# A relational graph layer on one core: the first weight's scale split in two halves, and its first half moved ahead of x's second tile

## The reference

```
h = relu(layernorm(x))                               # 1250 x 1024
u = h @ root + bias + sum over r of mean_r(h[src] by dst) @ weight[r]     # 8 relations
z = concat(u, h) @ w_gate + b_gate
out = x + tanh(u) * z + h * (1 - z)
```

## Time and profile before

| | us |
|---|---|
| median of 3 runs | 1406.08 |
| the three runs | 1405.66, 1406.08, 1414.51 |
| span of the profiled execution, from its first to its last instruction | 1407.7 |
| PE busy | 1291.5 (92%) |
| DVE busy | 952.5 (68%) |
| POOL busy | 754.8 (54%) |
| ACT busy | 409.0 (29%) |

### The profile page before, as it was taken

How to read it: one execution, slowest core, us unless ns; L and a number is a source line. 1 busy time by engine, 2 the same in 40 slices (tenths; PEclk the granted TensorE clock), 3 DMA queues, 4 the chain that set the end, 5 groups by cost and what they waited for, 6 DMA issues and landing times.

```text
span 1407.7 us, 20144 instructions
## 1 busy us (share of the span) xinstructions
PE 1291.5 (92%) x6205; PEld 651.6 (46%) x6205; DVE 952.5 (68%) x1260; ACT 409.0 (29%) x501; POOL 754.8 (54%) x837
## 2 busy tenths in 40 slices
PE   2978899999999999999998999998999989786898
PEld 1434344444444445555554445454445445343565
DVE  6889678366565667775675577646666778765777
ACT  5344123214132422321332043223222323432000
POOL 2423088786878426686687558664756464320000
PEclk9998899999999999999999999999999999998999
DMA  6442125215224348777875887769889977648872
GB/s 220 154 173 101 44 52 156 69 45 171 54 59 122 114 158 277 238 237 247 277 209 161 292 267 246 238 210 305 279 254 303 312 230 240 204 138 248 239 226 90
DMA packets 112355, 269.44 MB, mean 191 GB/s; under 512 B 22558, under 2 KB 23061, under 8 KB 112268
## 3 DMA queue, kind: packets, MB, share of 16 engines
q1 hardware_dynamic: 78284, 185.88, 40.2%
q0 software_dynamic: 33984, 82.40, 20.4%
HBM read 203.66 MB, written 87.30 MB: 207 GB/s over the span
## 4 chain that ended last, share of the span: by engine, by line
PE 61%; DVE 13%; DMA 10%; issue 7%; POOL 4%; ACT 2%; DVEq 1%; SPq 1%; POOLq 1%; ACTq 0%
PE ps L1320 52%; PE ps L1278 8%; DMA early<-y_rows,pair 7%; DVE W L937 2%; DMA early<-u_rows 1%; POOL onehot L641 1%; DVE hT L990 1%; DMA W<-in_L_gnn_weight_dram 1%; POOL early L633 1%; DVE hT L985 1%; PE ps L1313 1%; POOL pair L623 1%; DVE early L1147 1%; DVE early L1069 1%; DVE early L1163 1%
## 5 line engine op out<-in xcount | busy, mean ns | idle before, releaser
L1320 PE MATMUL ps<-W,hT 128*128 128x512 f16 (+2 forms) x4740 | 1076.0, 385 | 13.0 <-DVE W L937 13.0
L1320 PEld LDWEIGHTS ps<-W,hT 128*128 128x128 f16 (+2 forms) x4740 | 479.9, 104 | 537.8 <-issue 43.4
L633 POOL DMA_INDIRECT early<-y_rows,pair x200 | 242.1, 1211 | 194.5 <-PE ps L1281 152.4
L606 POOL DMA_INDIRECT table_rows<-edges,table_i x160 | 240.5, 1503 | 100.6 <-issue 100.6
L1278 PE MATMUL ps<-early,onehot 128*125 x800 | 205.9, 385 | 26.6 <-POOL onehot L641 13.1
L641 POOL TENSOR_SCALAR onehot<-iota_d,pair 128x125 f16<-128x125 f16 x185 | 159.9, 864 | 64.2 <-DMA early<-y_rows,pair 58.2
L766 ACT ACTIVATE yhl<-early 128x512 f16<-128x512 f32 x120 | 75.3, 628 | 355.3 <-DVE early L1069 194.2
L937 DVE SCALAR_TENSOR_TENSOR W<-W,wsc 128x2048 f16<-128x2048 f32 x62 | 146.5, 2364 | 13.8 <-ACT W L716 13.7
L1278 PEld LDWEIGHTS ps<-early,onehot 128*125 x800 | 106.8, 137 | 100.4 <-issue 46.6
L716 ACT ACTIVATE W<-W,wsc 128x2048 f16<-128x2048 f32 x62 | 122.6, 1990 | 50.9 <-DVE wsc L932 20.3
L683 ACT ACTIVATE peek_out<-W 128x1024 bf16<-128x1024 f32 x80 | 84.2, 1052 | 94.7 <-DMA W<-in_L_gnn_weight_dram 72.7
(11 more groups left out here) (184 smaller groups left out, 756.0 us busy)
## 6 DMA issues: line engine op xcount, KB each, us to landing
y_rows<-yhl SPq DMA_DIRECT2D x144, 256.0 KB
W<-in_L_gnn_weight_dram SPq DMA_DIRECT2D x31, 1024.0 KB, 7.4
early<-u_rows SPq DMA_DIRECT2D x52, 448.0 KB
u_rows<-early SPq DMA_DIRECT2D x50, 448.0 KB
W<-in_L_gnn_w_gate_dram SPq DMA_DIRECT2D x8, 1024.0 KB, 8.3
early<-in_x_dram SPq DMA_DIRECT2D x9, 512.0 KB, 4.5
hs_rows<-early SPq DMA_DIRECT2D x9, 512.0 KB, 3.2
u_rows<-yhl SPq DMA_DIRECT2D x18, 256.0 KB
```

What stands on the lines that cost most here:

```text
L606: pool.indirect_dma_start(out=table_rows, out_offset=bass.IndirectOffsetOnAxis(ap=at_i[:, c:c + 1], axis=0), in_=packed[0:EP, c:c + 1], in ...
L633: pool.indirect_dma_start(out=G[:, b, :], out_offset=None, in_=y_rows[i], in_offset=bass.IndirectOffsetOnAxis(ap=idx[:, b, :], axis=0), bo ...
L1320: last = nc.tensor.matmul(ps[0:rows, n % 4, :], hT[:, m, v_h, k, n0:n0 + rows], Wh[MAT[w][c]][:, v_w, k, :], start=(first and v_h + v_w == ...
```

## The change

The four quarters of the first weight (w = 0) are handled in two pairs. SyncE queues quarters 0 and 1 between x's tiles 0 and 1. Each pair has a scale of its own (a further slot in `wsc`; `scale_no` counts the scales: two for the first weight, one for each other). ScalarE, VectorE and TensorE go through tile 0 and the first pair, then through tile 1 and the second pair. ScalarE peeks at quarters 0 and 2, VectorE at 1 and 3. TensorE transposes tile 0, spreads the first pair's maximum and begins unit 0; tile 1's transposes and the second pair's maximum come behind unit 0. The first four units are now (0, 0), (1, 0), (0, 1), (1, 1) as (row tile, half). `add_group` for relation 0, whose product is that of the first weight, divides each half of the columns by its own scale.

```diff
-    ORDER = [[(j, h) for j in range(7) for h in range(2)] + [(j, 0) for j in range(7, NJ)] + [(j, 1) for j in range(7, NJ)],
+    ORDER = [[(0, 0), (1, 0), (0, 1), (1, 1)] + [(j, h) for j in range(2, 7) for h in range(2)] + [(j, 0) for j in range(7, NJ)] + [(j, 1) for j in range(7, NJ)],
...
-        inv = sb("inv", [P, 2], F32)
+        inv = sb("inv", [P, 4], F32)
-        wsc = sb("wsc", [P, NW, 3], I32)
+        wsc = sb("wsc", [P, NW + 1, 3], I32)
...
-        def wscale(w, c):
-            return wsc[:, w, c:c + 1].bitcast(F32)
+        def wscale(w, c, half=0):
+            return wsc[:, NW if w == 0 and half else w, c:c + 1].bitcast(F32)
+
+        def scale_no(w, half):
+
+            return half + 1 if w == 0 else w + 2
...
             load_x(0)
+            for q in range(2):
+                land(0, q)
             load_x(1)
-            for q in range(4):
+            for q in range(2, 4):
                 land(0, q)
... ScalarE
             def high_weights(w, c):
-                act.wait_ge(s["wscale_ready"], w + 1)
+                act.wait_ge(s["wscale_ready"], scale_no(w, c // 2))
...
-            for i in range(LEAD):
-                norm(i)
-            for i in range(LEAD):
-                turn_out(i)
+            norm(0)
             peek(0, 0)
-            peek(0, 1)
-            for c in range(4):
-                high_weights(0, c)
+            turn_out(0)
+            high_weights(0, 0)
+            high_weights(0, 1)
+            norm(1)
+            peek(0, 2)
+            turn_out(1)
+            high_weights(0, 2)
+            high_weights(0, 3)
... VectorE
-            def weight_top(w):
-                dve.wait_ge(s["peeked"], 4 + 8 * w)
+            def weight_top(w, half=1):
                 if w == 0:
-                    dve.wait_ge(s["peeked_first"], 4)
-                step(nc.vector.tensor_reduce(wtop[:, 0:1], wsum[:, w, :], AX.X, ALU.max))
+                    dve.wait_ge(s["peeked"], 2 + 2 * half)
+                    dve.wait_ge(s["peeked_first"], 2 + 2 * half)
+                    step(nc.vector.tensor_reduce(wtop[:, 0:1], wsum[:, 0, 4 * half:4 * half + 4], AX.X, ALU.max))
+                else:
+                    dve.wait_ge(s["peeked"], 4 + 8 * w)
+                    step(nc.vector.tensor_reduce(wtop[:, 0:1], wsum[:, w, :], AX.X, ALU.max))
...
+                if r == 0:
+                    step(nc.vector.tensor_scalar(inv[0:DT, 2:3], ps[0:DT, 6, 0:1], 1.0, wscale(0, 2, 1)[0:DT], ALU.max, ALU.mult))
+                    step(nc.vector.reciprocal(inv[0:DT, 3:4], inv[0:DT, 2:3]))
+                if r == 0:
+                    step(nc.vector.scalar_tensor_tensor(out=ub[0:DT, b, 0:HC], in0=ps[0:DT, 4, :], scalar=inv[0:DT, 1:2],
+                                                        in1=ub[0:DT, b, 0:HC], op0=ALU.mult, op1=ALU.add))
+                    nc.vector.scalar_tensor_tensor(out=ub[0:DT, b, HC:D], in0=ps[0:DT, 5, :], scalar=inv[0:DT, 3:4],
+                                                   in1=ub[0:DT, b, HC:D], op0=ALU.mult, op1=ALU.add).then_inc(s["u_added"], 1)
+                    return
...
-            for i in range(LEAD):
-                stats_of(i)
-            for i in range(LEAD):
-                turn_out(i)
-            first_peek(2)
+            stats_of(0)
+            first_peek(1)
+            dve.wait_ge(s["consts"], NCONST)
+            weight_top(0, 0)
+            weight_scale(0, 0)
+            turn_out(0)
+            stats_of(1)
+            low_weights(0, 0)
+            low_weights(0, 1)
             first_peek(3)
-            dve.wait_ge(s["consts"], NCONST)
-            weight_top(0)
-            weight_scale(0)
-            for c in range(4):
-                low_weights(0, c)
+            weight_top(0, 1)
+            weight_scale(0, 1)
+            turn_out(1)
+            low_weights(0, 2)
+            low_weights(0, 3)
... TensorE
             turn_h(0)
-            turn_h(1)
-            weight_max(0)
+            weight_max(0, 0)
             for n in range(NU):
...
+                if n == 0:
+                    turn_h(1)
+                    weight_max(0, 1)
```

More of the change, by code:

```diff
@@ L715, in high_weights @@
                 at = LAND[w][c if is_plain(w) else SOURCE[c]]
-                nc.scalar.activation(Wv[MAT[w][c]][:, 0, :], homes[at], ACT.Copy, scale=wscale(w, 0)).then_inc(s["w_hi"], 1)
+                nc.scalar.activation(Wv[MAT[w][c]][:, 0, :], homes[at], ACT.Copy, scale=wscale(w, 0, c // 2)).then_inc(s["w_hi"], 1)
             def norm(i):
@@ L921, in first_peek, with weight_scale @@
                                             AX.X, ALU.max, apply_absolute_value=True).then_inc(s["peeked_first"], 1)
-            def weight_scale(w):
-                dve.wait_ge(s["wall_ready"], w + 1)
+            def weight_scale(w, half=0):
+                dve.wait_ge(s["wall_ready"], scale_no(w, half))
                 step(nc.vector.tensor_reduce(wtop[:, 1:2], ps[:, 7, 0:P], AX.X, ALU.max))
@@ L931, in weight_scale @@
                 step(nc.vector.tensor_scalar(wexp[:, 2:3], wexp[:, 0:1], float(H_BITS - Y_BITS), None, ALU.add))
-                nc.vector.tensor_scalar(wsc[:, w, :], wexp[:, 0:3], 23, None, ALU.arith_shift_left).then_inc(s["wscale_ready"], 1)
+                nc.vector.tensor_scalar(wsc[:, NW if w == 0 and half else w, :], wexp[:, 0:3], 23, None, ALU.arith_shift_left).then_inc(s["wscale_ready"], 1)
             def low_weights(w, c):
@@ L936, in low_weights @@
                 at = LAND[w][c if is_plain(w) else SOURCE[c]]
-                nc.vector.scalar_tensor_tensor(out=Wv[MAT[w][c]][:, 1, :], in0=homes[at], scalar=wscale(w, 0),
+                nc.vector.scalar_tensor_tensor(out=Wv[MAT[w][c]][:, 1, :], in0=homes[at], scalar=wscale(w, 0, c // 2),
                                                in1=Wv[MAT[w][c]][:, 0, :], op0=ALU.mult,
@@ L1249, in turn_h, with weight_max @@
                     last.then_inc(s[turned], 1)
-            def weight_max(w):
-                pe.wait_ge(s["wtop_ready"], w + 1)
+            def weight_max(w, half=0):
+                pe.wait_ge(s["wtop_ready"], scale_no(w, half))
                 if turned_a[0]:
@@ L1261, in totals @@
                 pe.wait_ge(s["scan_ready"], SQ)
-                pe.wait_ge(s["wscale_ready"], 2)
+                pe.wait_ge(s["wscale_ready"], scale_no(1, 0))
                 nc.tensor.matmul(ps[0:EP, 7, P:P + NG], before[0:EP, 0:EP], scan3[:, :, EC - 1], start=True, stop=True)
```

## The result

Changed kernel: median 1412.9 us (20 runs, 1408.1 to 1419.9). Kernel before, in the same measurement: 1406.1 us (20 runs, 1399.9 to 1414.5). The ratio is 1.0043, 95% interval 1.0027 to 1.0058: 0.4% slower, some 6 us (3.8 to 8.2). That is within the 1% called no change, yet outside the noise of this many runs. The profiled execution took 1419.9 us (span 1418.2), 7 us over its median; that of before had a span of 1407.7, which with the same 1.7 around it is 3 us over. So the 10.5 us between the two spans aren't the change's price, and I read the stages instead.

The account below looks back on a forecast made before the run. Up to about 140 us, when VectorE leaves the four low-weight conversions was taken to bound the kernel. Leaving 2.6 us later plus 0.5 for relation 0's additions, on the 1406.1 median, gave 1409.2 us, range 1402.5 to 1415.

Parts of the forecast that it names:

- rival (c): Relation 0's ten additions all come onto TensorE's path, costing 5 us instead of 0.5: 1413.7 us; chance 13%.
- Transfers: At the start, x's tile 1 queued behind the second weight quarter, which then lands at about 10.4 us instead of 11.8.
- Rival (d): Second quarter still lands at 11.8 us because transfers share the engines; start 1.4 later, 1410.6 us; chance 10%.
- The reduce beside GpSimd's split: VectorE's two peek reduces take 2.3 us, ending at 12.7; 13.8 if held by GpSimd's split.
- First scale: Scale of the first weight's first pair, ready for ScalarE's first conversion at 15.5 us.
- TensorE's first half: After conversion of the first two quarters TensorE starts at 22.3 us, 7.4 us before its 29.74.
- Second product: Small product spreading the second half's maximum, queued behind unit 0 and tile 1's transposes: ready at 31.0 us.
- The relay: Chain across engines from tile 2's norm through edge keys to the scans, up to about 140 us: shifts by 2.6 us.
- Rival (b): In the relay, VectorE's 4.90 us cast L885 gets in ahead of GpSimd's split and memset: 1404.3 us; chance 12%.
- Rival (a): The early start survives, TensorE keeping its 7.4 us: 1398.7 us; chance 5%.
- I take 0.5 of the 5 on the path: Relation 0's ten additions each grow 0.5 us on VectorE, 5 us in all; only 0.5 reaches the total.
- between 520 and 700 never: TensorE never waited for relation 0's additions between 520 and 700 us; between 700 and 830 three times, 1.7 us.

Follow-up runs that it names:

- experiment 7: Changed kernel with the transfers queued in the old order, both tiles of x, then the four quarters; 1419.1 us, one run.
- experiment 3: Changed kernel with tile 1's transposes and the second half's maximum moved between unit 0's two row blocks; median 1410.5 us, ratio 1.0043.
- experiment 6: Kernel before, one scale and old order, with only tile 2's statistics and norm taken ahead; median 1400.2 us, ratio 0.9977.
- 8: experiment 6 with GpSimd's second pair of memsets moved up behind the first, out of the edge keys; median 1399.3 us, ratio 0.9943.
- experiment 2: Changed kernel with the short addition of before, one scale for both halves in relation 0, result partly wrong; median 1407.0 us, ratio 1.0014.
- 4: Changed kernel with tile 2's statistics and norm done in VectorE's wait for the second maximum; median 1409.1 us, ratio 1.0035.
- 5: Kernel of 4 with a shorter addition for relation 0, both scales in one operation, no wait between additions; median 1405.0 us, ratio 0.9992.
- 1: Kernel before with only relation 0's longer addition: second scale and reciprocal, two additions of 512 columns; median 1412.9 us, ratio 1.0058.

## Why the prediction was right, and where it wasn't

Direction and range held: 1409.2 forecast, 1412.9 measured, 1402.5 to 1415 stated. The number lies nearer to rival (c)'s 1413.7 than to the forecast, and is inside because the range was stretched to take in most of (c). The mechanism of the start held nearly instruction by instruction, and one term of the sum was mis-sized.

- Transfers. Second quarter at 10.4, measured 10.34 as the reduce's begin; experiment 7 confirms the 1.4 (1.5). Rival (d) falls.
- The reduce beside GpSimd's split: 10.34 to 12.69 beside a split from 9.45 to 11.58, 2.35 us for two, so it wasn't held. The Trainium skill's rule (SBUF — State Buffer, Who interferes with whom) that a tensor_reduce doesn't contend agrees with this row.
- First scale 15.5: 15.53. TensorE's first half 22.3: 22.31.
- Second product ready at 31.0, third high part at 32.35, statistics of tile 2 at 38.9: 31.4, 32.77, 39.34. From its begin to that of the next instruction unit 0 took 7.75 instead of the 7.2 of my sum: 0.2 of that I had misread (37.11 less 29.74 is 7.4 in the kernel before), the rest is when the clock rose. The transposes gave 0.16 back (0.90 from begin to begin, not 1.06). The delay is 3.0 instead of 2.6, and experiment 3 shows that it is the place of that product and nothing else.
- The relay. 3.03 at 62.72, 3.03 at 85.48, 3.03 at 134.79, 3.3 at 181.13: no slack, as forecast. Slow transposes of 1.03 and slow matmuls behind them (4.90 for twelve) came, and were covered. Rival (b) didn't occur: the cast L893 still took 4.89. Experiments 6 and 8 show that its kind of gain is to be had, but by moving work, not by luck.
- Rival (a), that TensorE keeps its 7.4 us: falls with experiment 6, which reaches the same stretch with the old start.
- **The step that failed** is "I take 0.5 of the 5 on the path". In the four other kernels with the long addition the sums slip by 3.4 to 4.0 us from the third to the 66th, in the changed kernel by 3.1. There the start plus the steps, 3.0 + 0.48 + 3.1 + a last 0.7 at the 68th, gives 7.3, against 6.7 between the medians (by the ratio 3.8 to 8.2). So the term is 4.3, not 0.5. Rival (c) had the mechanism and 13%. Two things were mis-sized. The addition grows by 0.70, not 0.5: two of 512 columns take 0.75 each with 0.04 between, where one of 1024 takes 1.28. And I compared it with the unit of 2.75 us between two sums, without what stands between an addition's end and TensorE's next sum. In experiment 2, whose addition is the short one, the numbers stand side by side:

```profile
531.99 0.22 DVE L1156 TENSOR_SCALAR inv<-ps,wsc 125x1 f32<-125x1 f32 x1 [0.99 <-issue]
532.24 0.17 DVE L1157 RECIPROCAL inv<-inv 125x1 f32<-125x1 f32 x1
532.44 1.28 DVE L1158 SCALAR_TENSOR_TENSOR early<-ps,inv,early 125x1024 f32<-125x1024 f32 x1
```

```profile
531.78 0.17 PE L1296 MATMUL ps<-ones_h,onehot 128*125 128x2 f16 x1
531.80 2.75 PE L1335 MATMUL ps<-W,hT 128*128 128x512 f16 x12
534.39 1.03 PE L1293 MATMUL ps<-early,onehot 128*125 x4
```

The addition ends at 533.72, TensorE comes to its next sum at 534.39: 0.67. Of that the hand-over, from the addition's end to the begin of a sum that waits for it, takes 0.4 (533.51 to 533.91 in the changed kernel's rows), so 0.27 are free, and an addition longer by 0.70 pushes the sum by 0.43; the step measured there was 0.48. The other places agree. At the 10th, 16th, 31st, 37th, 43rd and 52nd sum the kernel before has 0.61, 0.51, 0.41, 0.67, 0.66 and 0.67 from the addition's end to TensorE's next sum; less the 0.4 that leaves pushes of 0.5, 0.6, 0.7, 0.4, 0.4 and 0.4, and the steps were 0.55, 0.64, 0.66, 0.51, 0.49 and 0.48. At the 31st nothing was free: TensorE stood at the addition already in the kernel before, though the view of its waits names no addition before 745 us. Nor does the view show the size of such waits: in the changed kernel, where seven steps before 745 us make 3.8 us, it has from 520 us on 1.0 for the additions and 0.6 without a releaser:

```profile
PE ps L1302 <- DVE early L1164: 1.0, 2, 0.7
PE ps L1302 <- issue: 0.6, 2, 0.3
```

So my "between 520 and 700 never" was a reading of the view, not of the margin.

Open: the ratios put the additions at 4 us (the changed kernel against experiment 2), 6 (4 against 5) and 8 (1), each uncertain by some 3 to 5, the traces at 3.6 to 4.4 from the second to the 66th sum. Behind that the single traces differ by several microseconds either way (the difference of experiment 3 falls from +5.8 to -4.9 by the last sum), and what of it belongs to the additions wasn't settled. In experiments 1, 3, 4 and 5 the ratio comes out some 2 to 4 us above what the start and the steps of the trace add up to, which isn't explained.

## What to carry to other kernels

An engine that starts earlier gains only what it isn't made to wait for next: look up which unit the next hand-written wait sits in, and count what has been done by then in both versions. A small product on which another engine waits must not stand behind a long unit in an in-order queue; 4 us of VectorE hung on 0.4 us of TensorE. And a wait of zero in the trace isn't a margin: to lengthen a step, take the time from its end to its consumer's begin and subtract the hand-over, the shortest such time in the trace (0.4 us here).

## What the runs showed of the hardware

The same 24 matmuls of unit 0, behind a hole of 6 to 8 us, took 6.70, 7.04, 7.45, 7.48, 7.54, 7.91, 8.18 and 8.27 us in eight traces: the first 6 to 14 of them started some 0.43 us apart, the rest 0.216. That is 1.6 us of scatter in a stage from one execution to another. The clock column said 1.00 all the while, but it has no data there: the clock records of the traces begin only where the matmuls quicken (34.2 us in the kernel before, 27.6 in the changed one), so a 1.00 ahead of the first record says nothing. GpSimd's split of tile 1 took 4.07 us in the changed kernel, where it met VectorE's low-weight operation already running, instead of 2.12 as in the earlier trace rows; the holding goes both ways. And VectorE's cast of 125x160, 0.22 us by itself, took 4.89 beside a split and a memset one after the other: it didn't get in between them.
